# Placing 64 score-maxima products in an attention kernel: two a round in a shorter stretch, and the rest beside the experts' products

## What is computed

```python
xn = _layernorm(x)
q = (xn @ Wq) * mod;  k = (xn @ Wk) * mod;  v = (xn @ Wv) * mod     # 16 heads of width 8
scores = q @ k.T / sqrt(8) * cos(2 * pi * (i - j) / S)
w = softmax(scores);  w = (w + roll(w, 1)) / sqrt(2)
attention = (w @ v) @ Wo
# experts: 8, each token goes to the best two; per expert
he = silu(x @ w1a.T) * (x @ w1g.T) @ w2.T                           # 352 hidden columns
x = x + attention + experts(xn)
```

## Time and profile before

| | us |
|---|---|
| three runs, median (lowest to highest) | 611.27 (609.47 to 611.53) |
| the profiled execution, its own time | 609.38 |
| its span, first to last instruction | 607.6 |
| ScalarE busy, share of the span | 507.3, 83% |
| TensorE busy, share of the span | 541.1, 89% |
| VectorE busy, share of the span | 223.2, 37% |

### The profile page before, as it was taken

The page is one execution under the profiler, slowest core; times in us unless marked ns, Lnnn a source line. Parts: engine busy times, 40 slices in busy tenths (PEclk is TensorE's granted clock), DMA queues, the critical chain, the costliest instruction groups (busy, mean ns, idle before and its releaser), DMA issues.

```text
span 607.6 us, 18897 instructions
## 1 busy us (share of the span) xinstructions
PE 541.1 (89%) x7964; PEld 258.9 (43%) x7964; DVE 223.2 (37%) x521; ACT 507.3 (83%) x411; POOL 92.5 (15%) x102
## 2 busy tenths in 40 slices
PE   2979997877887789999999999999999999999984
PEld 1442333222222235554555554555454555545434
DVE  7866357345454533312231312231222222231234
ACT  2749988756566689999999998999999999999991
POOL 5210265431000001011011101011101111011100
PEclk9978999889789899999999999999999999999998
DMA  8851143350000503333343334243333233230042
GB/s 223 184 184 51 39 122 102 113 169 27 27 2 1 81 22 89 96 105 99 82 115 93 91 93 122 54 132 93 83 104 117 59 93 93 58 88 11 6 145 72
DMA packets 60889, 53.75 MB, mean 88 GB/s; under 512 B 33244, under 2 KB 50294, under 8 KB 60546
## 3 DMA queue, kind: packets, MB, share of 16 engines
q1 hardware_dynamic: 58082, 47.48, 29.4%
q0 software_dynamic: 2272, 4.72, 2.2%
q10 hardware_dynamic: 448, 0.30, 0.3%
HBM read 38.68 MB, written 13.78 MB: 86 GB/s over the span
## 4 chain that ended last, share of the span: by engine, by line
PE 42%; issue 24%; ACT 16%; DVE 11%; DMA 4%; SPq 2%; DVEq 0%; POOL 0%; ACTq 0%; POOLq 0%
PE ps L1387 19%; ACT big L695 15%; PE ps L1366 9%; DVE m L1054 4%; PE ps L1400 4%; PE ps L1309 4%; PE ps L1188 1%; DMA store<-results 1%; DVE store L778 1%; PE ps L1299 1%; ACT cs L687 1%; DMA qk_parts<-store 1%; DVE acc L1030 1%; PE ps L1199 1%; DMA acc<-in_L_attn_x 1%
## 5 line engine op out<-in xcount | busy, mean ns | idle before, releaser
L695 ACT ACTIVATE big<-ps 128x2048 f32<-128x2048 f32 x341 | 474.6, 1460 | 63.0 <-PE ps L1366 60.1
L1387 PE MATMUL ps<-big,vh 128*32 128x256 f32 (+1 forms) x3968 | 264.5, 399 | 0.2 <-ACT big L695 0.2
L1366 PE MATMUL ps<-qa,ka 49*128 49x512 f16 x896 | 154.1, 392 | 17.5 <-ACT big L695 9.1
L1387 PEld LDWEIGHTS ps<-big,vh 128*32 128x32 f32 x3968 | 113.0, 111 | 109.7 <-issue 56.1
L1366 PEld LDWEIGHTS ps<-qa,ka 49*128 49x128 f16 x896 | 34.0, 95 | 107.4 <-ACT big L695 73.2
L593 POOL DMA_INDIRECT results<-y,row_of x39 | 37.9, 973 | 258.1 <-DVE y L990 256.7
L975 DVE SCALAR_TENSOR_TENSOR cs<-cs,ps 128x384 f32<-128x384 f32 x39 | 21.6, 554 | 122.3 <-ACT cs L687 122.3
L1299 PE MATMUL ps<-xgT,store 128*32 128x128 f32 x1716 | 65.1, 273 | 0.1
L1054 DVE TENSOR_REDUCE m<-ps 128x1 f32<-128x512 f32 x64 | 44.2, 691 | 52.6 <-PE ps L1400 52.1
L1299 PEld LDWEIGHTS ps<-xgT,store 128*32 128x32 f32 x1716 | 54.0, 110 | 13.8 <-issue 0.6
L610 POOL DMA_INDIRECT slots_x<-attnT,slot x32 | 35.6, 1112 | 65.5 <-PE ps L1387 62.4
(11 more groups left out here) (189 smaller groups left out, 214.8 us busy)
## 6 DMA issues: line engine op xcount, KB each, us to landing
store<-in_L_ffn_w SPq DMA_DIRECT2D x39, 352.0 KB, 3.1
store<-in_L_ffn_w SPq DMA_DIRECT2D x39, 192.0 KB, 3.3
qk_parts<-store SPq DMA_DIRECT2D x8, 512.0 KB
qa<-qk_parts SPq DMA_DIRECT2D x27, 128.0 KB
slots_x<-vh SPq DMA_DIRECT2D x8, 330.0 KB, 7.3
cs<-slots_x SPq DMA_DIRECT2D x80, 32.0 KB, 2.8
store<-results SPq DMA_DIRECT2D x4, 512.0 KB, 5.6
ka<-qk_parts SPq DMA_DIRECT2D x31, 64.0 KB
```

The source lines that it names most:

```text
L695: nc.scalar.activation(probs[:, prob_of(tiles[0]):prob_of(tiles[-1]) + 1, :], ps[:, bank_of(tiles[0]):bank_of(tiles[-1]) + 1, :], ACT.Exp, ...
L1366: ins = nc.tensor.matmul(ps[:, bank_of(n), :], k[at:at + KQ, P * o:P * o + P], q[at:at + KQ, CW * c:CW * c + CW], start=True, stop=True, t ...
L1387: ins = nc.tensor.matmul(ps[32 * c:32 * c + 32, O_BANK, cols], vh[:, p % 2, o + 8 * b, :], probs[:, prob_of(n), cols], start=k == 0, stop= ...
```

## The change

The 64 jobs are placed anew. Jobs 0 to 35 stand two a round in rounds 27 to 44: the first behind both score groups, the second behind the values. Jobs 36 to 63 stand one a round in step 0 of the first 28 expert tiles, behind the score groups. The experts start at round 45 instead of 47, and end at round 162 instead of 164. Since experts and jobs now share the side bank in turn, a job beside them waits for `take_g` of the tile before (`hidT_ready`), and `widen` and `result` wait for the job's reduction. The shift of the exact heads is formed in round 129 and loaded in round 130. Of the second sums of squares, `key_weights` stays in round 19, `square_sums` goes to round 20, `turn_other` and `shifts` to round 22, `order_rest` and the loads of the exact heads' operands to round 23. Lines of the changed program are 11 to 17 higher for the same statement (L1387 is L1402, L1400 is L1417).

```diff
-JOBS_AT = 25
-JOBS_A_ROUND = 3
-JOBS_DONE = JOBS_AT + -(-JOBS // JOBS_A_ROUND)
-EXPERTS_AT = JOBS_DONE
+JOBS_AT = 27
+EXPERTS_AT = 45
+JOBS_BEFORE = 2 * (EXPERTS_AT - JOBS_AT)
+JOBS_BESIDE = JOBS - JOBS_BEFORE
+TURN_AT = EXPERTS_AT + ROUNDS_A_TILE * JOBS_BESIDE
-EXACT_AT = JOBS_DONE + 2
+EXACT_AT = TURN_AT + 1
...
         def jobs_of_round(r):
+            if JOBS_AT <= r < EXPERTS_AT:
+                j = 2 * (r - JOBS_AT)
+                return range(j, j + 1), range(j + 1, j + 2)
+            m, step = expert_step(r)
+            if step == 0 and m < JOBS_BESIDE:
+                return range(JOBS_BEFORE + m, JOBS_BEFORE + m + 1), range(0)
+            return range(0), range(0)
+        def jobs_beside(m):
+            return JOBS_BEFORE + min(m + 1, JOBS_BESIDE)
...
-                if r == SECOND_AT + 2:
+                if r == SECOND_AT + 4:
                     store_shifts(1)
...
                 m, step = expert_step(r)
-                for j in jobs[0:2]:
+                for j in jobs[0]:
                     take_max(j)
+                if r == TURN_AT:
+                    make_exact_shift()
...
                 if r == SECOND_AT:
                     key_weights(1)
+                if r == SECOND_AT + 1:
                     mean_squares(1)
                     dve.wait_ge(square_ready, 2)
                     other_of_second()
-                if r == SECOND_AT + 1:
+                if r == SECOND_AT + 3:
                     shifts(1)
-                if r == SECOND_AT + 2:
+                if r == SECOND_AT + 4:
                     order_rest()
...
-                    pe.wait_ge(exact_shift_ready, 1)
+                    pe.wait_ge(m_reduced, jobs_beside(0))
...
             def result(m):
                 pe.wait_ge(hidT_ready, m + 1)
                 after(pe, y_copied, m)
+                pe.wait_ge(m_reduced, jobs_beside(m + 1))
+                if m + 1 == JOBS_BESIDE:
+                    pe.wait_ge(exact_shift_ready, 1)
...
                 after(pe, m_reduced, j)
+                if m is not None:
+                    after(pe, hidT_ready, m)
...
                     scores(g)
-                    for j in jobs[g - 2 * r:g - 2 * r + 1]:
-                        max_job(j)
+                for j in jobs[0]:
+                    max_job(j, expert_step(r)[0])
+                if r == TURN_AT:
+                    turn_maxima()
...
-                if r == SECOND_AT:
+                if r == SECOND_AT + 1:
                     pe.wait_ge(slot_ready, 1)
                     square_sums(1)
-                if r == SECOND_AT + 1:
+                if r == SECOND_AT + 3:
                     turn_other(1)
                 for u in pieces:
                     weighted_values(u)
                 expert_work(r)
-                for j in jobs[2:]:
-                    max_job(j)
+                for j in jobs[1]:
+                    max_job(j, None)
```

More of the change, by code:

```diff
@@ L347, in jobs_of_round @@
         def jobs_of_round(r):
-            first = JOBS_A_ROUND * (r - JOBS_AT)
-            return range(first, min(first + JOBS_A_ROUND, JOBS)) if 0 <= first < JOBS else range(0)
+            if JOBS_AT <= r < EXPERTS_AT:
[7 more added lines that the diff above has]
+            return JOBS_BEFORE + min(m + 1, JOBS_BESIDE)
         def expert_step(r):
@@ L1108, in _ @@
                     rows_of_results()
-                for j in jobs[2:]:
+                for j in jobs[1]:
                     take_max(j)
-                if r == JOBS_DONE - 1:
-                    make_exact_shift()
             normalise(H - 1)
@@ L1389, in weighted_values, with max_job @@
                 ins.then_inc(pv_done, HALVES if k == 0 else 1)
-            def max_job(j):
+            def max_job(j, m):
                 h, i, c = job_at(j)
@@ L1405, in turn_maxima @@
                 pe.wait_ge(mx_ready, 1)
+                pe.wait_ge(hidT_ready, JOBS_BESIDE)
                 nc.tensor.transpose(ps[0:EXACT * NT, SIDE_BANK, 0:P], mx[:], ident[:]).then_inc(mxT_ready, 1)
@@ L1427, in _ @@
                 expert_work(r)
-                for j in jobs[2:]:
-                    max_job(j)
-                if r == JOBS_DONE - 1:
-                    turn_maxima()
+                for j in jobs[1]:
+                    max_job(j, None)
             project_all(0)
```

## The result

The changed kernel takes 581.93 us (median of 4 runs, 580.0 to 582.57) against 610.38 for the kernel before beside it: a ratio of 0.9528, 95% interval [0.9497, 0.9559], 4.7% faster. The profiled execution took 581.95 us, its span is 580.1.

What follows compares the result with a forecast made beforehand. Bound: TensorE 89% and ScalarE 83% busy, with job rounds and rounds 19 to 24 farthest above the floor. -25.2 - 4.2 + 9.1 - 0.4 = -20.7 from 609.38 gives 588.7; about half of 1.9 added: 589.5 us, range 581 to 600.

Steps and rivals of the forecast that it cites:

- rounds 25 to 46: Stretch of job rounds, 98.1 us before: forecast sum 72.9 with two plain rounds added at the end, so -25.2 us.
- The round with two jobs: Rounds with two jobs, 18 of them: 2.95 us each, between bounds of 2.66 and 3.21.
- the reductions hide: Two-job rounds: 1.17 fits in the values' 1.43; four and two tiles, about 1.0, leave at most 0.2 us.
- The formula with half of 0.53 absorbed by the wait for the small exponential: Two-job round: T = 2.68 + 0.53 - (T - 2.68), as that wait shrinks by the round's growth; T = 2.95 us.
- Head changes: At rounds 33 and 43: 4.6 us in all, each 1.2 and 1.1 for a late reduction.
- The 1.2 of a plain stretch: Cost of one head change, taken from rounds 19 to 24: 22.4 - 16.0 - 4.36 - 0.54 - 0.33.
- the 1.1 for late reductions: At each head change: 1.1 us for a job whose reduction stands behind the 0.69 us copy and the divisions.
- Job 0's wait and the half clock: At the first job: 3.1 us wait for the exact heads' operands, then 1.5 for one drop to half clock.
- Half clock in the stretch: Rounds 25 to 46: drops other than the one behind job 0's wait vanish; rival that half clock stays, 595, chance 0.12.
- Rounds 19 to 24: Rounds of the second sums, 22.4 us before: both waits and the 0.9 go, -4.2 us, bounds -2.5 and -5.
- Beside the experts: Expert rounds' step 0: 28 jobs at 0.30 us, 8.4, plus 0.7 for turning the maxima; +9.1 us.
- The end: Last copy: VectorE's adding of the experts' results goes off the path, -0.4 us.

Runs made afterwards that it cites:

- e4: Changed kernel with the reductions of jobs 0 to 35 over 256 of 512 columns: two-job rounds mean 2.84 us instead of 2.92; total of 6057 us not usable.
- e5: Changed kernel with both jobs of rounds 27 to 44 behind the groups of four and two, no values between: 591.49 us, ratio 0.9698 to before.
- e1: Kernel before with only the second sums of squares and the exact heads' loads moved: 610.45 us, ratio 1.0062 to before.
- e2: Changed kernel with the second sums of squares back in their old rounds: 581.88 us, ratio 0.9599 to before.
- e3: Changed kernel with jobs and experts starting two rounds later (29 and 47): 580.40 us, ratio 0.9554 to before.
- e7: Changed kernel with the product of each of the 28 jobs beside the experts issued twice: 587.85 us, ratio 0.9624 to before.

## Why the prediction was right, and where it was not

The time, 581.93, lies inside the range of 581 to 600, close to its edge; the forecast of 589.5 was a gain of 3.6% on 611.27, and 4.7% came. Four of the five stages came out lower than forecast and only the end higher; the largest miss is the 4.0 us of rounds 25 to 46.

- **The round with two jobs** was forecast at 2.95 and took 2.92, but not for the reason given. The step that failed is "the reductions hide": they do behind the values, not from the second job to the next first. Four and two tiles there take less than 1.17 us, and the job waits 0.30. The formula with half of 0.53 absorbed by the wait for the small exponential gave nearly the same number by chance. By the prediction's own signs this part was wrong: it allowed no wait over 0.2 us for a reduction, and named as a sign of error that jobs still wait for `m` in most rounds, which they do in every undisturbed round with two jobs. `e4` shows both limits: without the loop 2.84, with it 2.92; `e5` shows the loop as a whole.
- **Head changes** were mis-sized, the largest miss: 4.6 us forecast, 1.4 measured (rounds 33 to 36 and 44 take 2.68, 3.85, 2.93, 3.35 and 3.23 against 2.92 each). The 1.2 of a plain stretch, twice, was too much. It was what was left of 22.4 us after four subtractions, and with the 21.55 of the second profile of the same kernel the same subtractions leave 0.3. In the changed kernel a round with few values (33) gives 0.24 back, and round 34 costs 0.93. Of the 1.1 for late reductions only the one behind the divisions can be seen, 0.43 in round 36; the one behind the copy costs nothing more than the head change itself.
- **Job 0's wait and the half clock** were forecast at 3.1 + 1.5 and took 3.95. The copy ahead of the ranking came at 106.95 in an execution that was 2.1 us early at round 19, as forecast; the loads took 10.9 us from the end of the ranking (111.35 to 122.20) instead of 12.2.
- **Half clock in the stretch** went, as forecast: one spell of 3.4 us instead of 17.1 us in all in the first profile of before (in rounds 25 to 46), and the mean clock is 0.97 instead of 0.91. What the clock alone costs can be read from profiles with one order in rounds 26 to 46: 13.7 us at half clock and 91.82 us in the kernel before, 17.2 and 92.79 in its second profile, 6.8 and 89.67 in `e1`. That is about 1 us for a spell of 3.4, so by this estimate some 4 of the 29.2 us are the clock's, and the rest is the shorter rounds'.
- **Rounds 19 to 24**: -5.1 for -4.2, and against the second profile of before -4.2. Both waits and the half clock behind them went. What the prediction did not say, though its own terms hold it, is that this gain and the new wait at job 0 are one sum and nearly cancel: `e1` and `e2`.
- **Beside the experts**: 0.216 instead of 0.30 a job, 6.0 instead of 8.4 us. The 6.0 us that the prediction estimated by the Trainium skill, page "TensorE: Matmul & The Clock Gate", section "Wait — 56ns, not 53.3ns?", were right. The 0.32 of rows 4 contains the switch to the values, which is paid with or without the job: from the tiles to the values it is 0.98 without it and 1.20 with it (279.55 to 280.75). The 0.7 for turning the maxima can't be seen; instead 1.3 came in round 48, where VectorE's order put other work ahead of a reduction that TensorE now waits for. That wait was not foreseen.
- **The end**: the 0.4 is real as a wait (`e3` shows it coming back, 0.48), under a spread of 4 us in the last stage, so no total shows it.

## What to carry to other kernels

Where two engines pass one buffer to and fro, count the loop from product to product over the reader, and put enough of other work between two passes to cover it; where it stands counts as much as how many there are. Before you shorten a stage, look at what the stage behind it waits for: time taken from a wait comes back at the next one unless the chain that ends there is moved as well. And when a consumer begins to wait for an engine that was idle, read what else that engine has in its order just ahead of it.

## What the runs showed of the hardware

- TensorE's clock fell to 1.2 GHz without a long pause. In the kernel before it fell four times in the rounds with three jobs. Ahead of the first (123.2) stood pauses of 1.18 us and, for operands, of 1.04; ahead of the three others (160.8, 174.4, 208.6) the longest pause in 7 us was 0.57, 0.78 and 0.67 us, all of them waits for a reduction. The second profile shows the same three, and one more at 135.5 behind a pause of 0.75; `e1`, with the same order there, shows two of the three. In the changed kernel, where the rounds have one such wait of 0.30, it fell only behind the 2.27 us for operands. In `e5`, where the rounds have one wait of 0.57, it likewise fell only at the first job. In the expert rounds of either kernel it never fell.
- The last stage took from 17.0 to 21.0 us from one execution to another, mostly by how long half clock lasted in it (2.3 us in the 17.0, over 12 in the 21.0), and the first rounds took 55.3 to 57.6. A gain of less than 2 us shows in the stages of two profiles, not in the medians.
- A product of 512 columns issued behind one of its own shape in an expert round costs 0.216 us at full clock, the first (changed kernel) and the second (`e7`).
